# Moving half of one round's shared experts from the next round to the tail of a fused eight-sequence kernel

## The reference, cut to what matters

```python
logits = flat @ router_w.T                       # 64 experts, the best 4 of each token
xg = flat[tok_table]                             # up to 32 tokens for each expert
g = jnp.einsum('ecd,efd->ecf', xg, gate_w)
u = jnp.einsum('ecd,efd->ecf', xg, up_w)
y = jnp.einsum('ecf,edf->ecd', jax.nn.silu(g) * u, down_w)
out = jnp.zeros_like(flat).at[tok_table.reshape(-1)].add((y * w_table[..., None]).reshape(-1, d))
# the shared experts: every token, 2 x 256 hidden channels
sg = jnp.einsum('nd,sfd->nsf', flat, sh_gate_w)
su = jnp.einsum('nd,sfd->nsf', flat, sh_up_w)
out = out + jnp.einsum('nsf,sdf->nd', jax.nn.silu(sg) * su, sh_down_w)
...
x = x + _layernorm(out)
```

## Time and profile before

| | us |
|---|---|
| timed runs, median (range) | 1077.85 (1072.42 to 1078.45) |
| the profiled execution | 1075.03 |
| its span, first to last instruction | 1073.2 |
| mean granted TensorE clock | 0.985 of 2.4 GHz |

### The profile page before, as it was taken

One profiled execution on the slowest core, in us unless ns is written; L12 is line 12 of the kernel. 1 busy time (PEld: TensorE's weight loads), 2 busy tenths in 40 slices (PEclk: granted clock), 3 DMA queues, 4 the chain that ended last, 5 costly groups with the idle time before them and its releaser, 6 DMA issues.

```text
span 1073.2 us, 22270 instructions
## 1 busy us (share of the span) xinstructions
PE 1003.9 (94%) x8277; PEld 625.5 (58%) x8277; DVE 782.2 (73%) x1762; ACT 549.4 (51%) x1241; POOL 398.2 (37%) x617
## 2 busy tenths in 40 slices
PE   6999899899999999999999999999999999997985
PEld 3455556665454657765455657665455657765763
DVE  4889725779889765779889765778889645777436
ACT  3888621356888421356888421356888321441222
POOL 3466401133667111132666111142676001143742
PEclk9999999999999999999999999999999999999977
DMA  6889500003444100003434000003445903105577
GB/s 225 291 290 306 185 1 20 1 2 101 134 134 136 33 1 20 21 2 103 145 122 142 27 1 20 20 2 102 148 128 148 227 1 91 49 2 137 168 256 301
DMA packets 74748, 113.85 MB, mean 106 GB/s; under 512 B 6168, under 2 KB 64543, under 8 KB 73745
## 3 DMA queue, kind: packets, MB, share of 16 engines
q1 hardware_dynamic: 71952, 104.63, 31.4%
q0 software_dynamic: 1536, 3.60, 1.1%
q10 hardware_dynamic: 1152, 4.19, 1.0%
HBM read 93.60 MB, written 19.40 MB: 105 GB/s over the span
## 4 chain that ended last, share of the span: by engine, by line
PE 72%; DVE 12%; ACT 6%; issue 5%; POOL 2%; DMA 2%; SPq 1%; DVEq 0%; POOLq 0%; ACTq 0%
PE bank L1008 26%; PE bank L1110 5%; PE bank L1337 5%; PE bank L1218 4%; DVE hf L2026 3%; PE bank L1235 3%; PE bank L1125 2%; PE bank L1357 2%; PE bank L1450 2%; PE bank L1021 2%; DMA x<-cum_dram 2%; PE bank L1387 2%; PE bank L1502 1%; PE bank L1399 1%; PE bank L1411 1%
## 5 line engine op out<-in xcount | busy, mean ns | idle before, releaser
L1008 PE MATMUL bank<-uT,w_in 128*128 128x512 f32 (+1 forms) x584 | 272.8, 607 | 4.1 <-DVE hf L2040 3.5
L2026 DVE SCALAR_TENSOR_TENSOR hf<-bank,conv_w,hf 128x510 f32<-128x510 f32 (+2 forms) x224 | 162.5, 743 | 34.7 <-ACT nmax L1658 20.2
L1008 PEld LDWEIGHTS bank<-uT,w_in 128*128 128x128 f32 (+1 forms) x584 | 102.6, 188 | 124.3 <-issue 92.8
L1818 POOL TENSOR_TENSOR rs<-ve,half 128x2 f32<-128x2 f32 x56 | 39.6, 708 | 270.1 <-DVE ve L2216 270.1
L1641 ACT ACTIVATE hf<-bank,conv_b,conv_w 128x512 f32<-128x512 f32 x128 | 99.2, 775 | 50.5 <-PE bank L1008 50.1
L1008 PE MATMUL bank<-uT,w_gu 128*128 128x512 f32 x224 | 98.5, 593 | 0.0
L1218 PEld LDWEIGHTS bank<-hf 64*64 64x64 f32 x2048 | 74.1, 133 | 37.0 <-issue 31.7
L1218 PE MATMUL bank<-hf 64*64 64x128 f32 (+3 forms) x2048 | 88.2, 303 | 7.2 <-POOL hf L1881 3.7
L1619 ACT ACTIVATE xc<-bank 128x512 f32<-128x512 f32 x44 | 26.3, 597 | 98.9 <-PE bank L1008 71.9
L2518 DVE TENSOR_REDUCE nmax<-bank 128x2 f32<-128x256 f32 (+1 forms) x128 | 64.9, 553 | 13.5 <-PE bank L1441 12.9
L1008 PEld LDWEIGHTS bank<-uT,w_gu 128*128 128x128 f32 x224 | 42.3, 190 | 47.9 <-issue 47.4
(11 more groups left out here) (383 smaller groups left out, 2206.1 us busy)
## 6 DMA issues: line engine op xcount, KB each, us to landing
hf<-cum_dram SPq DMA_DIRECT2D x32, 384.0 KB, 3.5
dec<-cum_dram SPq DMA_DIRECT2D x32, 384.0 KB, 3.9
tmp<-cum_dram SPq DMA_DIRECT2D x32, 384.0 KB, 3.6
x<-cum_dram SPq DMA_DIRECT2D x32, 384.0 KB, 3.8
y_dram<-xf SPq DMA_DIRECT2D x16, 512.0 KB, 6.1
w_in<-in_w_in SPq DMA_DIRECT2D x1, 3584.0 KB, 11.4
w_in<-in_w_egu SPq DMA_DIRECT2D x6, 512.0 KB, 9.4
w_in<-y_dram ACTq DMA_DIRECT2D x5, 512.0 KB, 9.2
```

Of the source, the lines that this page charges most:

```text
L1008: mm = pe.matmul(plan[key][0:n, :], w[:, k, cols], uT[:, k, :], start=k == 0, stop=k == DC - 1)
L1818: pool.tensor_tensor(rs[:, cols], ve[:, cols], half[:, cols], ALU.pow).then_inc(rstd_ready.sem, 1)
L2026: ins = dve.scalar_tensor_tensor(d, x, conv_w[:, j, TAPS - 1 - s:TAPS - s], d, ALU.mult, ALU.add)
```

## The change

Half 1 of the shared experts of round 2 (`LATE`, tiles 10 and 11 of the 16) is not done in round 3 any more. Its tokens stay in `uT_moe`; round 3's own turned tokens go to `uT` instead. In round 3 the gate and up products (0, 1) and (1, 1), the down products of half 1, their Silus, gate products and copy are left out, and the store of round 2's sums has half the size.

In the tail, behind the last expert pair, TensorE's order is: identity products of sets 0 to 3, `late_hidden(0)`, the lane weights (now in bank 6), `late_hidden(1)`, then the sums; ahead of set 1 and of set 2 stand the down products of the two late tiles, which go straight into the bank of the final sums of set 5 (`late_down`), and the identity products of the other sets stand ahead of sets 2, 3 and 6. ScalarE has the two new Silus ahead of its waits for the scatters and its eight loads, VectorE the two gate products around the spreading of the lane weights. Two loads from `sh_dram` fall away. `yt` has two of its four buffers in `tmp` instead of `uT_moe`, with a wait for the last store of shared sums; three tiles of `shx` move out of the weights `w_sgu`.

```diff
+        def shared_in(r):
+            return SHARED if r < LAST else SHARED[:2]
+        def shared_halves(r):
+            return range(1) if r == LAST else range(2)
...
-                if f in (2, 5, 6):
+                if f in (2, 5, 6)[:len(shared_in(r)) - 1]:
                     keys.append(("SG", "SU", SHARED[1 + (2, 5, 6).index(f)]))
...
-        yt = [u[:, 2 * i:2 * i + 2, :] for i in range(2)] \
-            + [uT_moe[:, i, :].rearrange("p (g d) -> p g d", g=2) for i in range(2)]
+        yt = [u[:, 2 * i:2 * i + 2, :] for i in range(2)] + [tmp[:, 2 * i:2 * i + 2, :] for i in range(2)]
...
+        late_sg = xf[:, :, :].rearrange("p t d -> p (t d)").rearrange("p (g n) -> p g n", g=2)
+        late_shared = x1
+        LATE, LATE_SET = LAST - 1, ((LAST - 1) * TILES + 2) // 2
+        late_tiles = (2 * LATE_SET, 2 * LATE_SET + 1)
...
-        sums.use("lanes", 4)
+        sums.use("lanes", 6)
+        for g in range(2):
+            sums.use(("SG", g), 4)
+            sums.use(("SU", g), 5)
...
+                    if n == 0 and i in late_tiles:
+                        continue
                     sp.dma_start(shx[i][:, n, :], sums_dram[i * P:(i + 1) * P, :]).then_inc(shx_in[i // 4], 16)
...
+            def late_hidden(g):
+                for name, o in (("SG", 2 * g * P), ("SU", SHF + 2 * g * P)):
+                    pe.wait_ge(*sums.before((name, g), 0))
+                    for i in range(2):
+                        for k in range(DC):
+                            mm = pe.matmul(sums[(name, g)][:, i * HALF:(i + 1) * HALF],
+                                           w_sgu[:, k, o + i * P:o + (i + 1) * P], uT_moe[:, k, HALF:GROUP],
+                                           start=k == 0, stop=k == DC - 1)
+                    mm.then_inc(sums.fills((name, g)), 1)
+            def late_down(i):
+                if i == 0:
+                    for g in range(2):
+                        pe.wait_ge(*sums.drained(("SU", g), 0))
+                    pe.wait_ge(*sums.before(("SUM", LATE_SET), 0))
+                for f in range(SHF // P):
+                    pe.matmul(sum_of[late_tiles[i]], late_shared[:, f, i * P:(i + 1) * P], w_sdn[:, f, :],
+                              start=i == 0 and f == 0, stop=False, skip_group_check=True)
...
+            for q in range(4):
+                pe.wait_ge(*sums.before(("SUM", q), 0))
+                shared_set(q)
+            late_hidden(0)
             pe.wait_ge(spread_ready, ROUNDS)
             pe.wait_ge(*sums.before("lanes", 0))
...
             mm.then_inc(sums.fills("lanes"), 1)
...
-            for q in (0, 1, 2, 3, 6, 4, 5):
-                pe.wait_ge(*sums.before(("SUM", q), 0))
-                for i in sum_sets[q]:
-                    shared_rows(i, i == sum_sets[q][0])
+            late_hidden(1)
             pe.wait_ge(stat_ready, 2)
-            shared_rows(TOKENS // P - 2, True)
             for q, tiles in enumerate(sum_sets):
+                if q == 1:
+                    late_down(0)
+                if q == 2:
+                    late_down(1)
+                    shared_set(6)
+                if q == 3:
+                    pe.wait_ge(*sums.before(("SUM", 4), 0))
+                    shared_set(4)
+                    pe.wait_ge(*sums.drained(("SG", 1), 0))
+                    shared_rows(TOKENS // P - 2, True)
+                if q == len(sum_sets) - 3:
+                    pe.wait_ge(out_ready, 2)
+                    shared_rows(TOKENS // P - 1, True)
...
             expert_exp(LAST)
+            for g in range(2):
+                act.wait_ge(*sums.full(("SG", g), 0))
+                act.activation(late_sg[:, g, :], sums[("SG", g)][:, :], ACT.Silu).then_inc(sums.drains(("SG", g)), 1)
             for s in range(4):
                 act.wait_ge(y_out[s], 16 * EGROUPS // 4)
...
+                if p == 2:
+                    dve.wait_ge(sh_out, 16 * ROUNDS + CREDIT)
...
+            def late_gate(g):
+                dve.wait_ge(*sums.drained(("SG", g), 0))
+                dve.wait_ge(*sums.full(("SU", g), 0))
+                dve.tensor_tensor(late_shared[:, 2 * g:2 * g + 2, :],
+                                  late_sg[:, g, :].rearrange("p (f n) -> p f n", f=2),
+                                  sums[("SU", g)][:, :].rearrange("p (f n) -> p f n", f=2), ALU.mult)\
...
+            late_gate(0)
             dve.wait_ge(*sums.full("lanes", 0))
...
+            late_gate(1)
...
-                    if r > 0 and j == 0:
+                    if 0 < r < LAST and j == 0:
                         shared_up(1, 1, r - 1)
...
-                    if r > 0 and j == 1:
+                    if 0 < r < LAST and j == 1:
                         shared_down(1, r - 1)
```

More of the change, by code:

```diff
@@ L335, in sandwich @@
             if r > 0:
-                for n, gj in enumerate(SHARED[1:]):
+                for n, gj in enumerate(shared_in(r)[1:]):
                     plan.use(("SG", gj), 6, r - 1)
@@ L342, in sandwich @@
                         plan.use("pos", 6, r - 1)
-                for j in range(2):
+                if r == LAST:
+                    plan.use("table", 7, r - 1)
+                for j in shared_halves(r):
                     plan.use(("SD", j), 6 + j, r - 1)
@@ L493, in sandwich @@
         shx = [piece.rearrange("p (a d) -> p a d", a=2)
-               for home in (dec[:, :, :], turned_p[:, :, :], xc[:, :, :], sz[:, :, :], yg[:, :, :], w_sgu[:, :, :])
+               for home in (dec[:, :, :], turned_p[:, :, :], xc[:, :, :], sz[:, :, :], yg[:, :, :], w_out[:, :, :],
+                            att_rows[:, :, :], nmax[:, :, :, :].rearrange("p a i q -> p a (i q)"))
                for piece in pieces(home, 2 * D)]
@@ L512, in sandwich @@
         sums.base = [n + m for n, m in zip(tail.base, tail.count)]
-        sums.use("lanes", 4)
+        sums.use("lanes", 6)
+        for g in range(2):
+            sums.use(("SG", g), 4)
+            sums.use(("SU", g), 5)
         sum_sets = [(2 * q, 2 * q + 1) for q in range(TOKENS // P // 2 - 1)] + [(i,) for i in (TOKENS // P - 2, TOKENS // P - 1)]
-        for q in range(len(sum_sets) - 2):
-            sums.use(("SUM", q), (0, 1, 2, 3, 6, 7, 5)[q])
-        sum_of = {i: sums[("SUM", i // 2)][:, i % 2 * D:(i % 2 + 1) * D] for i in range(TOKENS // P - 2)}
-        sum_of[TOKENS // P - 2] = sums["lanes"][:, 0:D]
+        for q in range(len(sum_sets) - 3):
+            sums.use(("SUM", q), (0, 1, 2, 3, 5, 7)[q])
+        sum_of = {i: sums[("SUM", i // 2)][:, i % 2 * D:(i % 2 + 1) * D] for i in range(TOKENS // P - 4)}
+        for i in range(2):
+            sum_of[TOKENS // P - 4 + i] = sums["lanes"][:, i * D:(i + 1) * D]
+        sum_of[TOKENS // P - 2] = sums[("SG", 1)][:, 0:D]
         sum_of[TOKENS // P - 1] = sums[("SUM", 0)][:, 0:D]
@@ L619, in tail_tensor, with shared_rows, shared_set @@
                 down(p)
+            def late_hidden(g):
+                for name, o in (("SG", 2 * g * P), ("SU", SHF + 2 * g * P)):
+                    pe.wait_ge(*sums.before((name, g), 0))
+                    for i in range(2):
+                        for k in range(DC):
[11 more added lines that the diff above has]
+                              start=i == 0 and f == 0, stop=False, skip_group_check=True)
+            def shared_rows(i, first):
+                pe.wait_ge(shx_in[i // 4], 16 * (8 - 2 * (i // 4 == late_tiles[0] // 4)))
+                pe.matmul(sum_of[i], ident[:, :], shx[i][:, 0, :], start=first, stop=False, skip_group_check=True)
+            def shared_set(q):
+                for i in sum_sets[q]:
+                    shared_rows(i, i == sum_sets[q][0])
+            for q in range(4):
+                pe.wait_ge(*sums.before(("SUM", q), 0))
+                shared_set(q)
+            late_hidden(0)
             pe.wait_ge(spread_ready, ROUNDS)
@@ L766, in spread_weights @@
                                   .broadcast_to([P, TILES, TOPK, LANES]), ALU.mult).then_inc(spread_ready, 1)
+            def late_gate(g):
[4 more added lines that the diff above has]
+                                  sums[("SU", g)][:, :].rearrange("p (f n) -> p f n", f=2), ALU.mult)\
+                                      .then_inc(sums.drains(("SU", g)), 1)
             result_rows()
@@ L929, in store_shared @@
             def store_shared(r):
-                for j in range(2):
+                halves = shared_halves(r + 1)
+                for j in halves:
                     sp.wait_ge(*plan.drained(("SD", j), r))
                     settle(sp)
-                sp.dma_start(sh_dram[tok(r), :].rearrange("(t p) d -> p t d", p=P),
-                             tmp[:, :, :]).then_inc(sh_out, 16)
+                sp.dma_start(sh_dram[tok(r, HALF * len(halves)), :].rearrange("(t p) d -> p t d", p=P),
+                             tmp[:, 0:2 * len(halves), :]).then_inc(sh_out, 16)
             def ahead_x(r):
@@ L1073, in multiply_zeros, with turned_of @@
                 mm.then_inc(plan.drains(key, r), 1)
```

(4 more changed lines are left out.)

18 lines of the change are left out of this document (6 added, 12 removed).

## The result

| us | before | after |
|---|---|---|
| timed runs, median (range), 9 each | 1074.17 (1072.42 to 1078.45) | 1080.08 (1076.65 to 1084.68) |
| the profiled execution | 1075.03 | 1078.38 |
| its span | 1073.2 | 1076.6 |

The ratio is 1.0059, 95% interval [1.0043, 1.0076]: about 6.3 slower (5.9 by the medians), where no change was forecast (+0.8). The time lies in the range given; that the kernel would get measurably slower was not forecast.

The account below looks back on a forecast made before the run. TensorE was taken to bound round 3's FFN stage, row statistics its low-rank stage, VectorE the tail from the third set. -5.5 + 2.5 + 3.8 = +0.8 on 1075.03 gave 1075.8: forecast 1076, no change, range 1070 to 1082.

Parts of the forecast that it names:

- Round 3, removed work: Round 3: shared products taken out gain 5.18 in the FFN stage and 0.33 before the second half's transposes, sum -5.5.
- The hole: Round 3, before the attention's transposes: TensorE idles about 4.6, the clock falls, Q, K and first scores lose 2.5 (0 to 3.05).
- The short hole: Round 3, before the low-rank transposes at 904.08: about 1.4 of idle on TensorE, taken to cost nothing.
- the fourth rival: Round 3: the short hole also halves the clock over the low-rank products, +2.9, everything +3.7, 1078.7; chance 0.07.
- The tail: From the last expert products on: added late work and waits cost 1.1 + 0.2 + 2.5 = +3.8, bounds +1.3 and +4.4.
- The clock over the second late hidden products: Tail, behind the lanes: full clock taken, gate half ending at 1045.1 and up half at 1046.9.
- the third rival: Tail: lane products let the clock fall over the second late hidden products; tail +9.6, everything +6.6, 1081.6; chance 0.15.
- The landing of tile 0: Tail: first even load, issued from 1045.8 behind the second Silu, lands 4.8 later at 1050.6, after 3.7 of TensorE idle.
- From tile 0 to the third set: Tail: sums and late work from 1050.6 to third-set statistics at 1057.8, plus 2.5 for half clock after the wait.
- Behind it: Tail, after the third set's statistics: set 3 adds +0.2, then VectorE paces at 2.00 a set as before.
- The paying tail: Tail: even loads not held, tail -2.6, everything -5.6, or -8.1 with the clock up, 1069.4 to 1066.9; chance 0.08.
- the second rival: The paying tail: without held even loads, VectorE starts set 2's statistics 2.6 earlier than 1056.69; chance 0.08.

Follow-up runs that it names:

- e10: The changed kernel plus 20 products of zeros on TensorE behind the second late hidden products, in the wait for tile 0; ratio to the kernel before 1.0031.
- e1: The changed kernel with ScalarE's eight loads of the even tiles issued between its two late Silus instead of behind both; ratio to the kernel before 0.9989.
- e8: e1 with the late down and identity products spread out between the sets of sums; ratio to the kernel before 0.9968.
- e2: The changed kernel plus 18 products of zeros in round 3's hole ahead of the attention's transposes; ratio to the kernel before 1.0023.
- e4: The changed kernel with the lane products put two by two between the products of the first late hidden products; ratio to the kernel before 1.0052.
- e5: e9 with the lane products mixed two by two into the first late hidden products; ratio to the kernel before 0.9967.
- e7: The changed kernel with both late down products and the remaining identity products ahead of set 0, in the wait for tile 0; ratio to the kernel before 1.0016.
- e3: The changed kernel with the late half left out of the tail, so its output lacks the shared experts of tiles 10 and 11; ratio to the kernel before 0.9951.
- e9: e8 plus 18 products of zeros in round 3's hole, as in e2; ratio to the kernel before 0.9941, 1067.63 against 1074.40.
- e6: The changed kernel with all sixteen loads of routed results on SP's queue and the Silus unchanged; ratio to the kernel before 0.9991.
- e12: e9 with all sixteen loads on SP's queue; ratio to the kernel before 0.9954.
- e11: e5 with all sixteen loads on SP's queue; ratio to the kernel before 0.9943.

## Why the prediction was wrong

**Round 3, removed work: right.** From the FFN to the first transposes 5.18 was forecast; 891.26 against 897.33 is 6.07 less, of which 0.89 was there at the FFN (859.79 against 860.68): 5.18. To the second half's transposes (898.07) 0.33 was forecast, 0.27 measured; to the attention's nothing, 0.02 measured.

**The hole: right in kind, 0.3 too dear, and near by luck.** 2.5 was taken, 6.66 - 4.45 = 2.2 measured. The 2.5 is half of 5.1, the time from the resumed work at 974.76 to the clock's return at 979.9. But by the 0.73 of slice 976 the clock fell only at 976.5, so that example had half clock for 3.4 and a price of 1.7. In round 3 after, the clock was down before the work resumed at 911.64 and back at 916.8: another case, with 5.1 by chance. All of round 3 up to D: -3.3 measured, -3.0 forecast.

**The short hole: no price, as taken.** TensorE was idle 1.29 before 898.07, and the granted clock stayed at 1.00 up to 909. So the fourth rival did not come. The Trainium skill's rule beside it (page "TensorE: Matmul & The Clock Gate", section "A second HAM failure mode: psum-queue depth-cycling") is on frequent very short idles; one stretch of 1.29 gives it no support and does not test it either.

**The tail: right in its mechanism, too small by half.** +3.8 forecast, +7.6 measured. The order of the steps was as forecast (no idle behind D, lanes at full clock, loads behind the second Silu, a wait put down to a load, a clock that falls in it). The terms that were mis-sized, against D:

- *The clock over the second late hidden products: the step that failed first.* I took full clock up to their end at D + 13.9; the lanes let it fall at 1039.7 (0.83 in its slice), and the end came at D + 15.8. The second Silu began 1.7 late (D + 13.8 for 12.1) and the even loads 1.2 (D + 14.0 for 12.8): they went out 0.13 behind its start, not behind its 0.60. That is the third rival's start. It got 0.15; it deserved more, since the prediction's own row showed lanes that never brought the clock back. Its full price did not come: the clock was back at 1043, so the two falls stayed apart.
- *The landing of tile 0.* I took 4.8 from issue to landing, measured where both queues start together. After, it was 6.9 from the issue to the first sum (1042.75 to 1049.67). This is the largest miss, +2.1, and the second step that failed.
- *From tile 0 to the third set.* Forecast 7.2 at full clock (1050.6 to 1057.8) and 2.5 for the half clock; measured 7.85 (e10, 1048.80 to 1056.65) and 1.6. The half clock lasted 3.4 (1049.9 to 1053.3), like that behind 974.76 read rightly. The two errors cancel, which is luck: 9.7 forecast, 9.5 measured.
- *Behind it.* The third statistics to the end took 14.95 against 14.43: +0.5 where +0.2 was taken, and the last store 0.4 more.

Together 1.2 + 2.1 - 0.2 + 0.3 + 0.4 = 3.8, which is what was missing.

**The paying tail: priced too high.** e1 has what the second rival asks for, loads that are not held. It was to bring the third statistics 2.6 earlier than before the change; they came at D + 23.6 for 23.7. The half clock over the second late hidden products took 1.9 of that, the sums another 0.7 (7.85 for 7.2).

**Against which time: the second half of the miss.** The measured parts, -3.3 and +7.6, make +4.3; less the 0.9 that lay ahead of the change's first effect, they are the profiled pair's +3.4. The timed medians show 5.9. The median of 1077.85 that I had was one of three runs; nine gave 1074.17. I took the profiled execution of before (1075.03) as typical; in all later runs of before the median was 1073.9 to 1074.4, so it was about 0.9 above. And the after kernel's was 1.7 below its own median, at a higher mean clock than most of its runs. After spread over 8.0 in nine runs, before over 6.0; whether the added falls of the clock widen the spread is not shown. One trace is one draw from it.

## What to carry to other kernels

Before work is added in front of a DMA issue on a compute engine's queue, ask what that issue feeds: one Silu ahead of eight loads cost 7.5 here, and moving the loads, by two lines or to another queue, took it back. Work taken out of a stage leaves a hole where another chain sets the pace, and the hole has a price of its own: here keeping TensorE on wide products up to the first one that mattered (18 products of zeros in a hole of 4.6) gained 1.3 to 2.2 in the trace. And split what is inserted between paced steps: a piece and the step's own products should fit in the pace together. In e1, 2.8 of other work ahead of one set held VectorE up by 1.69; in e8 the pieces were 1.9 at most, which with the set's own 1.0 is still above the pace of 2.00 and held it up by 0.83, and the end came 1.9 earlier.

## What the runs showed of the hardware

**A queue whose loads went out while another was full got its first packets later.** DMA queues after, in the slice 1045 to 1046 (one row) and in the next (two): packets, MB, share of the 16 engines. q1 is SP's, q10 ScalarE's, whose loads had been issued from 1042.75 on.

```profile
q1 hardware_dynamic: 110, 0.41, 103.2%
...
q1 hardware_dynamic: 76, 0.25, 62.8%
q10 hardware_dynamic: 39, 0.16, 38.8%
```

q10 moved nothing for over 3.2 and then had its share. So it was in all six kernels whose even loads went out behind SP's (after, e2, e4, e5, e7, e10): the first packet 3.0 to 3.75 after the issue, the first load landed after 5.5 to 7.2. Where both went out together (before, e1, e3, e8, e9) the first packet came within 2.25, and the load landed after 4.8 to 5.1. The 5.5 is e2's, in which SP's queue had nothing left from 3.75 after ScalarE's issue. The Trainium skill, page "DMA: Bandwidth & Descriptors", section "Queues, rings and completion order", says that each engine takes turns between the queues that have work. The later slice agrees; the first, with q10 at nothing, fits only if that queue had no work for the engines yet, which no trace here shows. Where those 3.2 go stays open.

**One queue alone fills the engines:** q1 103.2% with 0.41 MB in 1.00 above, and e6's time is e1's.

**A run of 4-column products lets the clock fall, even from full clock.** It fell over the wide products right behind the lanes in every kernel with the late half that kept the 32 in one run (after, e1, e2, e6 to e10, e12), and in none that mixed them with wide ones (e4, e5, e11). The wide products took 5.39 in each of the nine and 4.13 for 18 records in the three.

**The same idle stretch does not always have the same effect.** The 2.77 behind the attention let the clock fall in twelve of the fourteen profiled executions and not in two. A fall that one trace shows is still a chance in the next execution.
